# Condition stage of a two-layer FFN/attention kernel: 32 tiles in one stream, score columns of both batches beside the value weights, first loads on two queues

## What is computed

```python
q = cond @ Wq.T + bq                    # one row for each batch
k = x @ Wk.T + bk
v = x @ Wv.T + bv                       # 16 heads of 32
scores = einsum('bhqd,bhkd->bhqk', q / sqrt(32), k)[:, :, 0, :]
attn = clip(scores, 0.0, 1.0)           # no softmax: each row stands alone
context = attn[..., None] * v
x1 = context @ Wo.T + bo
# two layers of local attention and FFN on x1, and at the end out = x + result
```

## Time and profile before

| | us |
|---|---|
| median of 3 runs | 3446.42 |
| lowest and highest run | 3445.81, 3451.23 |
| profiled execution, its own time | 3449.62 |
| span of the profiled execution | 3447.6 |
| PE busy | 3231.4 |
| DVE busy | 1763.0 |
| ACT busy | 1460.4 |
| POOL busy | 841.3 |

### The profile page before, as it was taken

One profiled execution on the slowest core, in us unless ns is written; L12 is line 12 of the kernel. 1 busy time (PEld: TensorE's weight loads), 2 busy tenths in 40 slices (PEclk: granted clock), 3 DMA queues, 4 the chain that ended last, 5 costly groups with the idle time before them and its releaser, 6 DMA issues.

```text
span 3447.6 us, 53475 instructions
## 1 busy us (share of the span) xinstructions
PE 3231.4 (94%) x19624; PEld 2641.9 (77%) x19624; DVE 1763.0 (51%) x3662; ACT 1460.4 (42%) x2957; POOL 841.3 (24%) x1472
## 2 busy tenths in 40 slices
PE   5995999999995999999996899999997899999999
PEld 5884788888884778877774688888885777777777
DVE  2553666666665434433333566666666533343333
ACT  1112777777773111111111677777775111111111
POOL 0003445444544100000001544444443500000000
PEclk9998999999997999999998999999998999999999
DMA  3223111111114211111113111111112311111110
GB/s 118 74 74 133 56 59 56 62 55 39 56 50 123 72 35 56 62 58 58 62 62 112 41 62 62 59 61 57 62 50 65 101 59 62 62 61 62 62 62 31
DMA packets 167416, 225.25 MB, mean 65 GB/s; under 512 B 25032, under 2 KB 94792, under 8 KB 166904
## 3 DMA queue, kind: packets, MB, share of 16 engines
q1 hardware_dynamic: 150264, 205.06, 18.1%
q10 hardware_dynamic: 16896, 16.78, 1.5%
HBM read 131.60 MB, written 60.83 MB: 56 GB/s over the span
## 4 chain that ended last, share of the span: by engine, by line
PE 91%; DVE 2%; issue 2%; DMA 1%; ACT 1%; POOL 1%; SPq 1%; POOLq 0%; DVEq 0%; ACTq 0%
PE bank L307 29%; PE bank L308 26%; PE bank L309 26%; PE bank L680 5%; PE bank L500 3%; PE bank L742 1%; DMA a_stage<-in_L_ffn_wqkv 1%; DVE a_PT_lo L1177 0%; DVE a_wq_lo L1194 0%; ACT a_P L910 0%; POOL a_qrot L1419 0%; ACT a_PT_hi L915 0%; DMA c_bo<-in_L_cond_bo 0%; DVE f_h L1279 0%; PE bank L517 0%
## 5 line engine op out<-in xcount | busy, mean ns | idle before, releaser
L307 PE MATMUL bank<-f_hT_hi,f_w_hi 128*128 128x512 f32 (+1 forms) x1408 | 560.0, 398 | 14.7 <-ACT f_hT_hi L982 14.7
L309 PE MATMUL bank<-f_hT_hi,f_w_lo 128*128 128x512 f32 (+1 forms) x1408 | 557.5, 396 | 0.0
L308 PE MATMUL bank<-f_hT_lo,f_w_hi 128*128 128x512 f32 (+1 forms) x1408 | 556.9, 395 | 0.0
L998 ACT ACTIVATE f_gate<-bank,f_b 128x512 f32<-128x512 f32 (+1 forms) x176 | 121.2, 689 | 1006.5 <-PE bank L309 1006.5
L1316 DVE SCALAR_TENSOR_TENSOR f_uraw<-bank,f_b,f_gate 128x512 f32<-128x512 f32 (+1 forms) x176 | 132.1, 750 | 718.3 <-ACT f_gate L998 718.1
L910 ACT ACTIVATE a_P<-a_S,a_bias 128x384 f32<-128x384 f32 x512 | 311.0, 609 | 246.8 <-DVE a_bias L1167 246.8
L1167 DVE CUSTOM_DVE_ANT_0 a_S<-bank,a_masks,a_q 128x384 f32<-128x384 f32 x512 | 295.0, 613 | 62.2 <-issue 45.5
L307 PEld LDWEIGHTS bank<-f_hT_hi,f_w_hi 128*128 128x128 f32 (+1 forms) x1408 | 260.8, 185 | 79.5 <-ACT f_hT_hi L982 15.4
L307 PE MATMUL bank<-a_PT_hi,a_V_hi 128*64 128x128 f32 x1536 | 304.7, 233 | 16.8 <-DVE a_PT_lo L1177 16.8
L309 PEld LDWEIGHTS bank<-f_hT_hi,f_w_lo 128*128 128x128 f32 (+1 forms) x1408 | 261.4, 186 | 67.7
L308 PEld LDWEIGHTS bank<-f_hT_lo,f_w_hi 128*128 128x128 f32 (+1 forms) x1408 | 261.3, 186 | 66.4
(11 more groups left out here) (164 smaller groups left out, 6956.9 us busy)
## 6 DMA issues: line engine op xcount, KB each, us to landing
a_h<-x_layer_in SPq DMA_DIRECT2D x128, 128.0 KB, 2.3
a_res<-x_layer_in SPq DMA_DIRECT2D x64, 256.0 KB, 2.9
x_after_attention<-out_tiles SPq DMA_DIRECT2D x64, 256.0 KB, 2.0
f_h<-x_after_attention ACTq DMA_DIRECT2D x32, 512.0 KB, 4.3
f_res<-x_after_attention SPq DMA_DIRECT2D x64, 256.0 KB, 3.6
f_x<-in_x SPq DMA_DIRECT2D x64, 256.0 KB, 3.1
x_layer_in<-f_res SPq DMA_DIRECT2D x64, 256.0 KB, 2.9
out<-f_res SPq DMA_DIRECT2D x64, 256.0 KB, 3.0
```

Of the source, the lines that this page charges most:

```text
L307: pe.matmul(dst, w[0], m[0], start=start, stop=False)
L308: pe.matmul(dst, w[0], m[1], start=False, stop=False)
L309: return pe.matmul(dst, w[1], m[0], start=False, stop=stop)
L998: act.activation(f_gate[0:ROWS[m], m % 2, :], bank[pair_of(u, m) + 1][0:ROWS[m], :], ACT.Gelu, bias=f_b1[0:ROWS[m], 1, m:m + 1]).then_inc( ...
```

## The change

It has these parts.

1. ACT, PE and DVE take the 32 tiles as one loop: on PE in step t stand x_T(t+1), v(t), ctx_T(t-1), o(t-2). Two of the banks trade places: x_T has bank 6, ctx_T bank 7, o banks 0 and 1.
2. `c_wv` has 8 more columns in each half: [scores of batch 0 | values | scores of batch 1]. The matmuls still take 264 columns, for batch 0 the first and for batch 1 the last. Nothing is rewritten between the batches.
3. The loads no longer wait for `started`. SP issues c_wq in four pieces, c_cond, ident, the first tile, c_bq, c_headmask, then c_wv_raw and the rest; ACT issues c_wk, c_bk, c_wo_raw. The semaphore `c_small_in` is split into `c_q_in` (three loads that q needs), `c_bk_in` and `c_bias_in`.
4. PE no longer waits for `started` before q. The first tile's transposes stand between q and A. DVE makes c_wv_lo before c_A, and c_wo_lo only in step 0 of the loop.
5. SP issues no loads past the last tile and waits for none. In the loop it issues the load first and the store of two tiles before after it.

The core of the diff:

```diff
@@ SP
-                sp.dma_start(ident[:], ident_dram).then_inc(ident_in, 16)
-                for r in range(QUAD):
-                    sp.dma_start(c_x[:, r, :], x_rows[r * P:(r + 1) * P, :]).then_inc(c_x_in[r], 16)
-                sp.dma_start(c_wq[:], wqT.rearrange("(k p) n -> p k n", p=P)).then_inc(c_wq_in, 16)
...
+                for k in range(KT_):
+                    sp.dma_start(c_wq[:, k, :], wqT[k * P:(k + 1) * P, :]).then_inc(c_wq_in, 16)
+                    if k == 0:
+                        sp.dma_start(c_cond[:], cond).then_inc(c_q_in, 16)
+                sp.dma_start(ident[:], ident_dram).then_inc(ident_in, 16)
+                sp.dma_start(c_x[:, 0, :], x_rows[0:P, :]).then_inc(c_x_in[0], 16)
+                sp.dma_start(c_bq[:], bq.rearrange("(k p) -> p k", p=P)).then_inc(c_q_in, 16)
+                sp.dma_start(c_headmask[:], headmask_dram.rearrange("p (k h) -> p k h", k=KT_)).then_inc(c_q_in, 16)
+                sp.dma_start(c_wv_raw[:], wvT.rearrange("(k p) n -> p k n", p=P)).then_inc(c_wv_in, 16)
...
+                sp.wait_ge(started, 1)
+                for t in range(TILES):
+                    if t + QUAD < TILES:
+                        sp.wait_ge(c_xT_mm, START + t + 1)
+                        sp.dma_start(c_x[:, t % QUAD, :], x_rows[(t + QUAD) * P:(t + QUAD + 1) * P, :])\
+                          .then_inc(c_x_in[t % QUAD], 16)
+                    if t >= 2:
+                        store(t - 2)
+                store(TILES - 2)
+                store(TILES - 1)
...
-                for j in range(QUAD):
-                    sp.wait_ge(c_x_in[j], START + (BLOCKS + 1) * 16)
@@ PE
-                        x_T(0)
...
-                        x_T(1)
-                        v(0)
-                        x_T(2)
-                        v(1)
-                        ctx_T(0)
-                        x_T(3)
-                        v(2)
-                        ctx_T(1)
-                        o(0)
-                        v(3)
-                        ctx_T(2)
-                        o(1)
-                        ctx_T(3)
-                        o(2)
-                        o(3)
+                def x_T(t):
+                    pe.wait_ge(c_x_in[t % QUAD], START + (t // QUAD + 1) * 16)
+                    pe.wait_ge(c_xT_lo, START + t)
+                    transpose_tile(bank[6], c_x[:, t % QUAD, :]).then_inc(c_xT_mm, 1)
...
+                for t in range(TILES + 2):
+                    if t + 1 < TILES:
+                        x_T(t + 1)
+                    if t < TILES:
+                        v(t)
+                    if 0 <= t - 1 < TILES:
+                        ctx_T(t - 1)
+                    if t >= 2:
+                        o(t - 2)
@@ ACT
+                act.dma_start(c_wk[:], wk.rearrange("(k p) n -> p k n", p=P)).then_inc(c_wk_in, 16)
+                act.dma_start(c_bk[:], bk.rearrange("(k p) -> p k", p=P)).then_inc(c_bk_in, 16)
+                act.dma_start(c_wo_raw[:], woT.rearrange("(k p) n -> p k n", p=P)).then_inc(c_wo_in, 16)
+                act.wait_ge(started, 1)
@@ DVE
+                for t in range(TILES + 2):
+                    if t + 1 < TILES:
+                        x_T(t + 1)
+                    if t == 0:
+                        dve.wait_ge(c_wvo_hi, START + 2)
+                        dve.tensor_tensor(c_wo[1][:], c_wo_raw[:], c_wo[0][:], ALU.subtract).then_inc(c_wvo_lo, 1)
+                        dve.wait_ge(c_bias_in, START + 2 * 16)
+                    if t < TILES:
+                        context(t)
+                    if 0 <= t - 1 < TILES:
+                        ctx_T(t - 1)
+                    if t >= 2:
+                        o(t - 2)
```

More of the change, by code:

```diff
@@ L324, in condition @@
[L324 to L328, removed]
@@ L524, in condition @@
                 mm.then_inc(c_A_mm, 1)
[L525 to L564, removed]
-                                mm = three_passes(pe, bank[6 + j % 2][:],
-                                                  [c_ctxT[i][:, j % 2, k, :] for i in range(2)],
-                                                  [c_wo[i][:, k, :] for i in range(2)], k == 0, k == KT_ - 1)
-                            mm.then_inc(c_o_mm, 1)
-                        x_T(0)
-                        pe.wait_ge(c_Ab_hi, START + b + 1)
-                        pe.wait_ge(c_Ab_lo, START + b + 1)
@@ L821, in condition @@
                         for half in range(2):
-                            cp = act.activation(c_wv[0][:, :, half, 0:HALF],
+                            cp = act.activation(c_wv[0][:, :, half, CA:CA + HALF],
                                                 c_wv_raw[:, :, half * HALF:(half + 1) * HALF], ACT.Copy)
                     else:
+                        act.wait_ge(c_A_set, START + 1)
+                        for b in range(B):
+                            for half in range(2):
+                                a_part = act.activation(c_wv[0][:, :, half, b * (CA + HALF):b * (CA + HALF) + CA],
+                                                        c_A[:, :, b * CH + half * CA:b * CH + (half + 1) * CA], ACT.Copy)
@@ new lines, in x_T, with ctx_T @@
+                def x_T(t):
+                    act.wait_ge(c_xT_mm, START + t + 1)
+                    if t >= 2:
+                        act.wait_ge(c_v_mm, START + 2 * (t - 1))
+                    act.activation(c_xT[0][:, t % 2, :, :], bank[6][:].rearrange("p (k n) -> p k n", k=KT_),
+                                   ACT.Copy).then_inc(c_xT_hi, 1)
+                def ctx_T(t):
+                    act.wait_ge(c_ctxT_mm, START + t + 1)
+                    if t >= 2:
+                        act.wait_ge(c_o_mm, START + t - 1)
+                    act.activation(c_ctxT[0][:, t % 2, :, :], bank[7][:].rearrange("p (k n) -> p k n", k=KT_),
+                                   ACT.Copy).then_inc(c_ctxT_hi, 1)
@@ L859, in attention @@
+                for t in range(TILES + 1):
+                    if t + 1 < TILES:
+                        x_T(t + 1)
+                    if t >= 1:
+                        ctx_T(t - 1)
             def attention(l):
@@ new lines, in condition, with x_T @@
+                        c0 = b * (CA + HALF)
+                        lo = dve.tensor_tensor(c_wv[1][:, :, half, c0:c0 + CA],
+                                               c_A[:, :, b * CH + half * CA:b * CH + (half + 1) * CA],
+                                               c_wv[0][:, :, half, c0:c0 + CA], ALU.subtract)
+                lo.then_inc(c_Ab_lo, 1)
+                def x_T(t):
+                    dve.wait_ge(c_xT_hi, START + t + 1)
+                    dve.tensor_tensor(c_xT[1][:, t % 2, :, :], bank[6][:].rearrange("p (k n) -> p k n", k=KT_),
+                                      c_xT[0][:, t % 2, :, :], ALU.subtract).then_inc(c_xT_lo, 1)
```

223 lines of the change are left out of this document (99 added, 124 removed).

## The result

The changed kernel takes 3412.32 us (median of 5 runs, 3411.38 to 3413.96) against 3446.42 us, a ratio of 0.9899 with a 95% interval of 0.9888 to 0.9910. That is 34.1 us less, where 36.6 were predicted (3409.8); it lies inside the range. The profiled execution took 3413.96 us with a span of 3412.1, 35.5 less than the span of before, where the sum by rows gave 36.6. All medians and ratios in this document are of the fast executions; one execution of e4 (9142.79 us) and one of e9 (5381.11 us) were slow, for a reason that nothing here shows, and are left out.

The account below looks back on a forecast made before the run. PE was taken to bound the kernel, its idle stretches being where time can be won. Terms of 12.2 + 4.4 + 18.9 + 1.1 = 36.6 us took the median from 3446.4 to 3409.8, range 3402 to 3421.

Parts of the forecast that it names:

- Term 1: Condition stage's steady stream: one loop removes PE's wait at seven block borders, 12.2 us less, bounds 11.3 and 12.5.
- 4.6 us of cover: Steady stream: DVE has c_xT_lo ready 4.6 us before PE's next transposes need it, so no new wait comes.
- stall rival: Steady stream: c_xT_lo comes late behind out_tiles on DVE, so PE waits every step; 3466 at 8.4 us a step; 4 in 100.
- Term 2: Chain from first matmul to first v: 18.6 us instead of 22.98, 4.4 us less.
- Term 3: Start of the first matmul: loads issued at 0.8, start at 12.0 instead of 30.9, 18.9 us less; bounds 7.5 and 15.2.
- the two readings: c_headmask's landing: its old delay of 11.35 us, and 2.8 MB under equal queue shares, both giving about 11 us.
- Term 4: Stage's end, last store to first a_h load: 2.6 instead of 3.8 us, 1.1 us less.
- No early start: Kernel's beginning: engines start later than POOL or DMAs are held, first matmul at 23.4, total 3421; 7 in 100.
- The pieces one after another: Loads for q: c_wq's four pieces are served in turn, first matmul at 18.5, total 3416; 5 in 100.
- The stream gives nothing: Steady stream: a short wait in every tile replaces that at each fourth, 7.03 us a step, total 3422; 4 in 100.
- held by DVE: Steady stream: x_T(t+1) finds c_xT_lo(t) not ready on DVE; 3466 at 8.4 us a step; 4 in 100.
- The rule on the second queue: Initial loads: the Trainium skill says a second issuing engine adds no bandwidth and saves only issue time.

Follow-up runs that it names:

- e4: The kernel before, with only SP's loads issued without waiting for started, in the old order on one queue: 3435.74 us, ratio 0.9969.
- e9: The changed kernel with x_T of tiles 4, 8, ... 28 put back at the end of the step before, on PE, ACT and DVE: 3422.33 us.
- e6: The changed kernel with DVE making c_xT_lo of the next tile behind context instead of ahead of it: 3418.20 us, ratio 0.9916.
- e5: The changed kernel with DVE making c_xT_lo of the next tile last in each step, behind out_tiles, instead of first: 3467.70 us, ratio 1.0059.
- e2: The changed kernel with ACT's three loads (c_wk, c_bk, c_wo_raw) given back to SP's queue: 3403.59 us, ratio 0.9872.
- e10: The changed kernel with only c_wo_raw moved from ACT's queue to the end of SP's loads: 3408.46 us, ratio 0.9887.
- e1: The changed kernel with SP, ACT and PE again waiting for started before their first DMA or matmul: 3423.20 us, ratio 0.9924.
- e3: The changed kernel with c_wq loaded by one DMA of 1 MB instead of four of 256 KB: 3412.11 us, ratio 0.9896.
- e12: The changed kernel with c_wq and q's other loads divided over the heads of both queues, c_c's copy off the path: 3408.52 us, ratio 0.9884.

## Why the prediction was right, by its steps

- **Term 1, the stream, 12.2.** From the first v to the last store's issue: 279.38 - 53.88 = 225.5 before, 245.19 - 32.86 = 212.3 after, 13.2 less, beyond the upper bound of 12.5. A tile takes 6.57 or 6.58 where 6.59 was read off PE's timeline, which gives 12.7 for seven heads, and no new wait came. About 0.4 is from the first v, which the prediction left alone: it took 4.74 us (32.86 to 37.60) in place of 5.13 (53.88 to 59.01), with 17 of its 24 matmuls at half pitch in place of 21. The heads of before follow each other at 28.13 us, the one between the two batches too, so the rewriting of the score columns cost PE nothing of its own. e9 shows that the seven heads are the gain. The claim of 4.6 us of cover was tested from both sides: 4.2 of them used up leave the full step alone (e6), and past it the stall rival's mechanism appears (e5), with steps of 8.24 us and 3467.70 where the rival had 3466 for steps of 8.4.
- **Term 2, the chain to the first v, 4.4.** 32.86 - 14.38 = 18.48, where 18.6 was summed; 4.5 less. Each part stood within 0.2 us of where it was put.
- **Term 3, the first matmul, 18.9.** Measured 30.90 - 14.38 = 16.5. This is the term that was mis-sized, by 2.4. The issue at 0.8 was right (0.72); the landing was not. The step that failed is "if both get equal shares, about 2.8 MB must move": 4.1 MB had moved. ACT's 2 MB passed in whole, as e2 and e10 show by taking them away one by one, and some 0.6 MB of SP's later loads passed too. The second part could have been read from the rows of before: up to 23.0 us its slices hold 3.1 MB, while 2.2 MB stood ahead of c_headmask. So the two readings that met at 11 us were not the same thing: one set the landing at the bytes ahead, the other had 0.9 MB more in it. With that surplus added, 3.7 MB at the slices of before are reached near 24.9 us and give a start near 14. That the start still lay below the upper bound of 15.2 is in part luck: the 4.1 MB came in 13.7 us from the first issue, 0.30 MB for each us, and at the 0.27 of before (3.1 MB in 11.35 us) they would have taken until about 16.
- **Term 4, the end, 1.1.** 3.80 against 2.38: 1.4 less.
- **The sum.** 13.2 + 4.5 + 16.5 + 1.4 = 35.6 for 36.6. Term 3's miss of 2.4 was more than half made up by the others, which is luck: they erred by 1.4 together, the other way. The rest of the difference, 1.5 us between 35.6 at the stage's end and 34.1 in the medians, is between the runs and not behind the stage: what follows the stage took 3164.4 and 3164.5 us in the two profiles, while the profiled execution was 3.2 above the median before and 1.6 above it after.
- **The rivals.** No early start: refuted by the trace and e1. The pieces one after another: refuted by the changed kernel's own start at 14.38, not 18.5, and by e3, where one large DMA wins 1.2 us and not 6.5. The stream gives nothing, or is held by DVE: refuted for this kernel by its waits, the second shown to be real by e5.
- **The rule on the second queue**, which was weighed as changing nothing, was the place to look harder, though for what the second queue takes and not for what it adds: a reading in which the needed loads go alone was a bound there (start at 7.5), and one queue gives it (8.20).

## What to carry to other kernels

- When a first matmul waits for loads, count everything that is queued on any queue before these loads' last byte, and keep what isn't needed yet behind them. A second queue added early traffic and cost 6.2 us here; the same bytes on one queue, in the order of need, came in time. Two queues cost nothing at the first matmul when what it needs heads both (8.39 in e12).
- Read an engine's own work per tile off its timeline between two like instructions (6.59 here), not from the named wait: the bracket of 1.5 to 1.6 us stood for a hole of about 1.8.
- In a software pipeline the cover of a late operation is the step's length, and the first steps are shorter than the full ones. An operation moved back may be free in the loop and still cost at its start.

## What the runs showed that I had not expected

- Loads on ACT's queue passed ahead of SP's last needed load in whole, which then landed 3.0 us later for the first megabyte and 3.2 for the second (8.20, 11.23, 14.38).
- Bytes queued behind a load on its own queue also moved before it had landed: about 0.9 MB before the change, 0.6 MB after it.
- The work behind the condition stage, unchanged in all kernels, took from 3159.7 (e9) to 3169.2 us (e3) in the profiles. A part is in attention's beginning: from the first a_h load to the first a_OT_hi 81.1 to 84.1 us, where PE waits for weights and changes between its two clock levels (granted clock 0.50 to 1.00 in stretches of 10 us). The larger part is further on, between the first and the last a_OT_hi: 2284.0 to 2289.6 us. What makes it vary is not shown. A gain of a few us ahead of such a stretch can't be read from one run's total.
